# Small inputs of a one-core transformer kernel laid out by the host, and zero products ahead of the first real ones

## What is computed

```python
mod = (silu(c) @ wmod).reshape(16, 6, 1, 128)              # sa, ca, ga, sb, cb, gb
h = layernorm(x) * (1 + ca) + sa
h = sqrt(128) * h + pos
for l in range(4):
    n = layernorm(h) * ln1_s[l] + ln1_b[l]
    q, k, v = n @ Wq[l] + bq[l], n @ Wk[l] + bk[l], n @ Wv[l] + bv[l]
    h = h + linear_attention(elu(q) + 1, elu(k) + 1, v) @ Wo[l] + bo[l]
    n = layernorm(h) * ln2_s[l] + ln2_b[l]
    h = h + relu(n @ W1[l] + b1[l]) @ W2[l] + b2[l]
x = x + ga * (layernorm(h) * lnf_s + lnf_b)
x = x + gb * experts(layernorm(x) * (1 + cb) + sb)         # 8 experts, top 2, and a shared one
```

## Time and profile before

| | us |
|---|---|
| median of 3 runs | 573.39 |
| lowest, highest | 573.23, 573.44 |
| the profiled execution, its own time | 575.53 |
| its span in the profile | 573.4 |
| PE busy in the span | 555.7 (97%) |
| DVE busy | 440.4 (77%) |
| ACT busy | 394.9 (69%) |
| POOL busy | 261.4 (46%) |

### The profile page before, as it was taken

The page is one execution under the profiler, slowest core; times in us unless marked ns, Lnnn a source line. Parts: engine busy times, 40 slices in busy tenths (PEclk is TensorE's granted clock), DMA queues, the critical chain, the costliest instruction groups (busy, mean ns, idle before and its releaser), DMA issues.

```text
span 573.4 us, 13217 instructions
## 1 busy us (share of the span) xinstructions
PE 555.7 (97%) x4572; PEld 532.5 (93%) x4572; DVE 440.4 (77%) x1543; ACT 394.9 (69%) x1395; POOL 261.4 (46%) x431
## 2 busy tenths in 40 slices
PE   5899999999999999999999999999999999999997
PEld 3488899999999999998999999998999999999896
DVE  4877777778986777777997777778897667667795
ACT  2877978786666666786594765787676666666651
POOL 4344668454323446654503526646313435336420
PEclk9989999999999999999999999999999999999999
DMA  7700254000000000000000000000000000000000
GB/s 223 225 5 1 67 188 181 5 1 2 21 1 20 1 2 2 1 2 2 2 19 21 1 1 2 1 2 1 2 19 19 2 2 1 2 2 1 2 19 18
DMA packets 11049, 15.60 MB, mean 27 GB/s; under 512 B 960, under 2 KB 8224, under 8 KB 10600
## 3 DMA queue, kind: packets, MB, share of 16 engines
q1 hardware_dynamic: 8904, 12.54, 7.1%
q0 software_dynamic: 448, 1.25, 0.8%
q10 hardware_dynamic: 1632, 0.98, 0.6%
HBM read 12.63 MB, written 2.14 MB: 26 GB/s over the span
## 4 chain that ended last, share of the span: by engine, by line
PE 86%; ACT 5%; DVE 5%; POOL 1%; issue 1%; DMA 1%; DVEq 0%; SPq 0%; POOLq 0%
PE psA L1624 21%; PE psD L1624 19%; PE psB L1624 19%; PE psC L1624 19%; PE psB L1696 1%; PE psC L1696 1%; PE psD L1696 1%; PE psA L1696 1%; DMA wm<-in_wmod 1%; ACT L524 1%; ACT L478 1%; PE psA L1747 1%; PE psB L1747 1%; PE psC L1747 0%; PE psD L1747 0%
## 5 line engine op out<-in xcount | busy, mean ns | idle before, releaser
L843 POOL TENSOR_TENSOR rstdD<-msD,neghalf 128x2 f32<-128x2 f32 x20 | 14.0, 699 | 53.8 <-ACT ziD L470 41.7
L1624 PE MATMUL psC<-w,H 128*128 128x128 f32 x256 | 34.2, 276 | 0.5 <-ACT H L493 0.5
L1624 PE MATMUL psB<-w,H 128*128 128x128 f32 x256 | 33.1, 275 | 0.0
L1624 PE MATMUL psA<-w,H 128*128 128x128 f32 x256 | 33.0, 275 | 0.0
L1624 PEld LDWEIGHTS psC<-w,H 128*128 128x128 f32 x256 | 31.1, 192 | 1.5 <-ACT H L493 1.5
L1624 PE MATMUL psD<-w,H 128*128 128x128 f32 x256 | 31.8, 275 | 0.0
L1624 PEld LDWEIGHTS psB<-w,H 128*128 128x128 f32 x256 | 30.9, 192 | 0.0
L1624 PEld LDWEIGHTS psA<-w,H 128*128 128x128 f32 x256 | 30.8, 192 | 0.0
L1624 PEld LDWEIGHTS psD<-w,H 128*128 128x128 f32 x256 | 30.3, 192 | 0.0
L470 ACT ACTIVATE eqkA<-xA 128x129 f32<-128x129 f32 x64 | 19.3, 307 | 11.4 <-DVE xA L1190 10.5
L843 POOL TENSOR_TENSOR rstdA<-msA,neghalf 128x2 f32<-128x2 f32 x20 | 14.6, 732 | 26.8 <-ACT eqkA L470 23.0
(11 more groups left out here) (587 smaller groups left out, 2403.9 us busy)
## 6 DMA issues: line engine op xcount, KB each, us to landing
M<-modulation_rows SPq DMA_DIRECT2D x2, 1280.0 KB, 9.1
M<-modulation_rows SPq DMA_DIRECT2D x1, 2560.0 KB, 8.8
out<-X SPq DMA_DIRECT2D x16, 128.0 KB, 1.9
M<-in_attn_W SPq DMA_DIRECT2D x3, 256.0 KB, 3.6
X<-in_attn_x_in ACTq DMA_DIRECT2D x2, 256.0 KB, 3.6
M<-in_attn_W ACTq DMA_DIRECT2D x1, 256.0 KB, 3.7
wo<-in_attn_Wo POOLq DMA_DIRECT2D x1, 256.0 KB, 4.7
wm<-in_wmod SPq DMA_DIRECT2D x1, 256.0 KB, 4.3
```

The source lines that it names most:

```text
L843: pool.tensor_tensor(b.rstd[:, :], b.ms[:, :], neghalf[:, :], ALU.pow).then_inc(b.s_rstd.sem, 1)
L1624: return pe.matmul(o, lhsT, rhs, start=start, stop=stop)
```

## The change

The host now lays out the small inputs: the condition and the six parameter tables as one transposed table of 128 x 40 (`small`), the four biases joined, the last norm's scale and shift joined, the four weights of each layer joined to 896 columns, W2 with its partition first. The two transpositions on PE, the copy of `parT` on DVE and the waits for them go; `c_in` and `parT` are parts of `small`. PE begins with six products of a tile of zeros with itself (`idle_passes`), which write to a bank that is overwritten later. The arithmetic is otherwise the same.

```diff
+        small = sb("small", [P, BATCH + 6 * LAYERS])
+        c_in, parT = small[:, 0:BATCH], small[:, BATCH:]
...
+        w_all = last_rows[:, 0:LAYERS * (QKV + FF)].rearrange("p (l n) -> p l n", n=QKV + FF)
+        wqkv, w1 = w_all[:, :, 0:QKV], w_all[:, :, QKV:]
...
+        zeros = CD[1].att[:, 0, :]
...
         def _(sync):
-            sync.dma_start(c_in[:, :], cond).then_inc(s_k, 16)
-            sync.dma_start(K[:, 0:C_FIRST], consts[:, 0:C_FIRST]).then_inc(s_k, 16)
+            sync.dma_start(small[:, :], small_in).then_inc(s_k, 16)
             sync.dma_start(wm[:, 0:2 * D], wmod[:, 0:2 * D]).then_inc(s_wm, 16)
-            for n, a in enumerate((ln1_s, ln1_b, ln2_s, ln2_b, bo, b2)):
-                sync.dma_start(par[n * LAYERS:(n + 1) * LAYERS, :], a).then_inc(s_par, 16)
+            sync.dma_start(K[:, 0:C_FIRST], consts[:, 0:C_FIRST]).then_inc(s_ident, 16)
             sync.dma_start(cen, consts[:, C_CEN:]).then_inc(s_par, 16)
...
+            sync.dma_start(bias[:, :, :], bias_in.rearrange("(a l) n -> a l n", a=1).to_broadcast([2, LAYERS, QKV + FF]))\
+                .then_inc(s_bias, 16)
             tiles_in = x_in.rearrange("b (t p) f -> p (b t) f", p=P)
             k = CHAINS * TILES
+            sync.dma_start(Xv[:, k // 2:k, :], tiles_in[:, k // 2:k, :]).then_inc(s_xfirst[1], 16)
+            sync.dma_start(K[:, C_FIRST:C_CEN], consts[:, C_FIRST:C_CEN]).then_inc(s_pos, 16)
+            sync.dma_start(wm[:, 2 * D:], wmod[:, 2 * D:]).then_inc(s_wm2, 16)
+            sync.dma_start(lnf, lnf_in.rearrange("(a n) -> a n", a=1).to_broadcast([BATCH, 2 * D])).then_inc(s_lnf, 16)
+            for l in range(1, LAYERS):
+                sync.dma_start(w_all[:, l, :], w_in[:, l, :]).then_inc(s_weights[l], 16)
+                if l == 1:
+                    sync.dma_start(w2[:, :, :, :].rearrange("p l c n -> p (l c) n"), w2_in).then_inc(s_w2in, 16)
...
         def _(act):
             tiles_in = x_in.rearrange("b (t p) f -> p (b t) f", p=P)
-            for n in range(2):
-                k = slice(n * 2 * TILES, (n + 1) * 2 * TILES)
-                act.dma_start(Xv[:, k, :], tiles_in[:, k, :]).then_inc(s_xfirst[n], 16)
-            for n, a in enumerate((Wq, Wk, Wv)):
-                act.dma_start(wqkv[:, 0, n * D:(n + 1) * D], a[0, :, :]).then_inc(s_wqkv[0], 16)
-            act.dma_start(w1[:, 0, :], W1[0, :, :]).then_inc(s_w1[0], 16)
+            act.dma_start(Xv[:, 0:2 * TILES, :], tiles_in[:, 0:2 * TILES, :]).then_inc(s_xfirst[0], 16)
+            act.dma_start(w_all[:, 0, :], w_in[:, 0, :]).then_inc(s_weights[0], 16)
 
             def condition():
 
-                act.wait_ge(s_parps, 1)
-                act.activation(condT[:, :], A.ps[:, 1, 0:BATCH], ACT.Silu).then_inc(s_condT, 1)
+                act.wait_ge(s_k, 16)
+                act.activation(condT[:, :], c_in, ACT.Silu).then_inc(s_condT, 1)
...
         def _(pool):
+            pool.memset(zeros, 0.0).then_inc(s_zero, 1)
             pool.memset(neghalf[:, :], -0.5).then_inc(s_const, 1)
...
         def _(dve):
 
-            def parameters():
-
-                dve.wait_ge(s_parps, 2)
-                dve.tensor_copy(parT[:, :], A.ps[:, 1, 0:6 * LAYERS]).then_inc(s_parT, 1)
-                dve.wait_ge(s_parT, 1)
-
             def fold_matrix(n):
 
                 l, k = n // 2, n % 2
+                dve.wait_ge(s_k, 16)
+                dve.wait_ge(s_ident, 16)
...
-            def condition():
-
-                pe.wait_ge(s_k, 32)
-                pe.transpose(A.ps[:, 1, 0:BATCH], c_in[:, :], ident[0:BATCH, 0:BATCH]).then_inc(s_parps, 1)
-
-            def parameters():
-
-                pe.wait_ge(s_condT, 1)
-                pe.wait_ge(s_par, 112)
-                pe.transpose(A.ps[:, 1, 0:6 * LAYERS], par[:, :],
-                             ident[0:6 * LAYERS, 0:6 * LAYERS]).then_inc(s_parps, 1)
+            def idle_passes(n):
+
+                pe.wait_ge(s_zero, 1)
+                for _ in range(n):
+                    mm(D_.ps[:, 0, 0:D], zeros, zeros)
 
             def bias_rows(k):
 
                 if k == 0:
-                    pe.wait_ge(s_parT, 1)
+                    pe.wait_ge(s_k, 16)
+                    pe.wait_ge(s_par, 16)
...
-                pe.wait_ge((s_wqkv, s_w1)[k][min(l, 1)], (48, 16)[k] * (1 if l == 0 else LAYERS - 1))
-                pe.wait_ge(s_bias, 64)
+                pe.wait_ge(s_weights[l], 16)
+                pe.wait_ge(s_bias, 16)
...
-            condition()
+            idle_passes(6)
             first_rows(D_)
             first_rows(B)
             first_rows(C)
             first_rows(A)
-            parameters()
             bias_rows(0)
```

More of the change, by code:

```diff
@@ L38 @@
 ENTRY_PE = (3, 1, 2, 0)
-ENTRY_DVE = (2, 0, 1, 3)
 ROUTE_STEPS = 14
@@ L101, in of, with program @@
         return self.value(i, names.index(name) + 1)
-def program(nc, x_in, Wq, bq, Wk, bk, Wv, bv, Wo, bo, W1, b1, W2, b2, ln1_s, ln1_b, ln2_s, ln2_b, lnf_s, lnf_b,
-            router, e_gate, e_up, e_down, s_gate, s_up, s_down, cond, wmod, consts, select, out, rows):
+def program(nc, x_in, Wo, router, e_gate, e_up, e_down, s_gate, s_up, s_down, wmod, small_in, bias_in, lnf_in, w_in,
+            w2_in, consts, select, out, rows):
     nc.disable_value_cache = True
@@ L271, in program @@
         s_spread = [sem(f"spread{n}") for n in range(len(SPREAD))]
-        s_wqkv, s_w1 = [sem("wqkv"), sem("wqkvrest")], [sem("w1in"), sem("w1rest")]
+        s_weights = [sem(f"weights{l}") for l in range(LAYERS)]
         s_wo, s_w2in, s_wmoe = sem("wo"), sem("w2in"), sem("wmoe")
@@ L279, in program @@
         s_parps = sem("parps")
-        s_parT = sem("parT")
+        s_ident = sem("ident")
         s_bplus = sem("bplus")
         s_inmod = sem("inmod")
-        s_factor = sem("factor")
+        s_zero = sem("zero")
         s_condT = sem("condT")
@@ L339, in _ @@
             sync.dma_start(cen, consts[:, C_CEN:]).then_inc(s_par, 16)
-            sync.dma_start(K[:, C_FIRST:C_CEN], consts[:, C_FIRST:C_CEN]).then_inc(s_pos, 16)
-            for n, a in enumerate((bq, bk, bv)):
-                sync.dma_start(bias[:, :, n * D:(n + 1) * D],
-                               a.rearrange("(a l) n -> a l n", a=1).to_broadcast([2, LAYERS, D])).then_inc(s_bias, 16)
-            sync.dma_start(bias[:, :, QKV:], b1.rearrange("(a l) n -> a l n", a=1).to_broadcast([2, LAYERS, FF])).then_inc(s_bias, 16)
@@ L2169, in _, with laid_out @@
                     expand(B, i + 1, 0, 0)
-_INS = ["attn_x_in", "attn_Wq", "attn_bq", "attn_Wk", "attn_bk", "attn_Wv", "attn_bv", "attn_Wo", "attn_bo",
-        "attn_W1", "attn_b1", "attn_W2", "attn_b2", "attn_ln1_s", "attn_ln1_b", "attn_ln2_s", "attn_ln2_b",
-        "attn_lnf_s", "attn_lnf_b", "ffn_router", "ffn_experts_gate", "ffn_experts_up", "ffn_experts_down",
-        "ffn_shared_gate", "ffn_shared_up", "ffn_shared_down", "c", "wmod"]
+_INS = ["attn_x_in", "attn_Wo", "ffn_router", "ffn_experts_gate", "ffn_experts_up", "ffn_experts_down",
+        "ffn_shared_gate", "ffn_shared_up", "ffn_shared_down", "wmod"]
+def laid_out(get):
+    small = [get("c")] + [get("attn_" + n) for n in ("ln1_s", "ln1_b", "ln2_s", "ln2_b", "bo", "b2")]
+    w2 = get("attn_W2").reshape(LAYERS, CH, P, D).transpose(2, 0, 1, 3)
+    return {"in_small": np.concatenate(small, axis=0).T,
+            "in_biases": np.concatenate([get("attn_" + n) for n in ("bq", "bk", "bv", "b1")], axis=1),
+            "in_lnf": np.concatenate([get("attn_lnf_s"), get("attn_lnf_b")]),
+            "in_weights": np.concatenate([get("attn_" + n) for n in ("Wq", "Wk", "Wv", "W1")], axis=2).transpose(1, 0, 2),
+            "in_w2": w2.reshape(P, LAYERS * CH * D)}
 def build(nc, inputs):
@@ L2181, in build @@
         arrays["in_" + name] = np.ascontiguousarray(inputs["L0_" + name])
+    for name, a in laid_out(lambda name: inputs["L0_" + name]).items():
+        arrays[name] = np.ascontiguousarray(a)
     arrays["in_consts"] = constants()
```

34 lines of the change are left out of this document (10 added, 24 removed).

## The result

| | before | changed |
|---|---|---|
| median of 6 executions each, us | 573.89 (573.23 to 575.09) | 582.25 (578.61 to 584.05) |
| ratio to before, 95% interval | | 1.0131 (1.0106 to 1.0155) |
| profiled execution: time, span, us | 575.53, 573.4 | 581.0, 578.8 |

The changed kernel is slower: by 8.4 us by the medians, by 7.5 us by the ratio. A comparison leaves out executions that lie over 1.5% above the fastest of the same kernel, here four of the fourteen of `e9` and one of the kernel before (921.17 us, beside `e9` to `e12`).

The account below looks back on a forecast made before the run. PE, 97% busy, was taken as the bound, the gain as time off the chain ahead of about 26 us: 2.0 - 0.5 (clock) = 1.5 us off 575.53 us, 574.0 us, then 2.14 us to the median: 571.9 us, range 570.4 to 574.2 us.

Parts of the forecast that it names:

- Weights of the modulation: Start of the kernel: `wm`, moved to second on SP, lands at 4.4 to 5.2 us, so `first_rows` starts before 5.77 us.
- Removed on PE and DVE: Ahead of the first fold: two transpositions and the `parT` copy go; PE is through at 12.15 us even with low clock.
- DVE's start is the new limit: Tiles of C and D, sixth on SP, land at 6.2 to 7.0 us; first fold starts at 12.5 instead of 13.86 us.
- late-transfers rival: SP's queue: tiles land only at 7.9 us beside ACT's long rows, leaving 0.2 us of gain, 573.2 us; chance 0.12.
- The clock's term: PE's waits up to the first fold: a clock fall there costs 0 to 1.1 us, taken as 0.5 us.
- The slower rival: PE ahead of the first fold: clock stays low until past 18 us, giving 574.6 to 576.3 us; chance 0.13.
- The sum: Whole program: 2.0 us gain less 0.5 us for the clock gives 574.0 us, then 2.14 us to the median, 571.9 us.
- The rest costs nothing: Idle passes, memset of zeros, SP issues, W2's rows and new waits, mostly at the start: no cost.

Follow-up runs that it names:

- e9: Changed kernel with transfers ordered by when they are first read, tiles of C and D back on ACT; 573.01 us over all 14 executions, ratio 0.996.
- e12: Kernel before with the tiles of C and D issued late on SP and zero products in PE's later waits; 577.06 us, ratio 1.0047.
- e1: Changed kernel without its six opening zero products; 583.52 us, ratio 1.016.
- e15: Changed kernel with fourteen zero products ahead of the first fold only; 575.11 us, ratio 1.0024.
- e3: Changed kernel with zero products in two PE waits, 6 ahead of modulation(0) and 16 ahead of the first fold; 575.32 us, ratio 1.0025.
- e6: Kernel before with only late zero products (2, 2 and 5) in PE's later waits, no layout change; 573.21 us, ratio 0.9992.
- e13: e10 without the six opening zero products; 572.38 us, ratio 0.997.
- e10: e9 with late zero products (2, 2 and 5) in PE's later waits; 572.45 us, ratio 0.9975.
- e5: Changed kernel with tiles of C and D on ACT and zero products in PE's waits, both ahead of the first fold and later; 573.61 us, ratio 0.9986.
- e8: Changed kernel with layer 0's joined weights moved from ACT to SP, behind the tiles of C and D; 580.72 us, ratio 1.0114.
- e2: Changed kernel with the tiles of C and D back on ACT's queue, ahead of the joined weights; 574.64 us, ratio 1.0007.

## Why the prediction was wrong

It said 571.9 us and at most 574.2 us; 582.25 us came. By its own steps:

- *Weights of the modulation*, 4.4 to 5.2 us: right, 4.38 us. *Removed on PE and DVE*: right, the two transpositions and the copy are gone. PE was free at 10.1 us instead of 12.15 us, since the clock rose at 5.4 us and not "by 8 us". That looked like a gift; it made the wait ahead of the fold longer. It is not a condition of the fall, though: in e1 the clock rose at 8 us, and it fell all the same.
- *DVE's start is the new limit*: the mechanism was right, DVE works gapless from the tiles to `bias_plus_one`. Its size was not: the tiles landed at 7.7 us, outside 6.2 to 7.0 us and near the late-transfers rival's 7.9 us. The fold started at 13.6 us instead of 12.5 us. The estimate took the 3.2 to 4.0 us of transfers that stood second and third in SP's queue; the sixth took 4.7 us. With this step wrong and the clock up, e15, the time is 575.11 us, 1.3 us above the kernel before, and not the small gain that the rival gave; why, the fifth point says.
- ***The clock's term* is the step that failed.** It put the end of the range at 1.1 us, on the ground that the clock would be back by the second fold. The low level stayed for 10.2 us, with PE busy for 8.79 us of them, and a second stretch of 6.8 us followed; together they cost some 6 us (e15's trace against the change's). The price was there in the rows: the same four products take 2.08 us low and 1.14 us high, so 8.79 us of low work are, by estimate, some 4 us too many. I bounded the stretch by the one low stretch that the trace had (3.4 us) and by the rise 5.3 us after 10.03 us; neither says how long a fall after a wait of 3.5 us lasts. The Trainium skill, page "TensorE: Matmul & The Clock Gate", section "HAM oscillation — how this bites in real kernels", prices a low stretch at half the duration of its products. The traces agree for the first stretch: half of 8.79 us is 4.4 us, and e15 is 4.3 us ahead at `fold_weights(2)`; for both stretches the rule gives 7.8 us and the traces some 6 us. e3 and e15 keep the tiles late and fill the wait: about 7 of the 8.4 us are gone by the medians, 6.1 of 7.5 us by the ratios.
- *The slower rival* had the place (PE, between `modulation(0)` and the fold) and the sign (the clock low past 18 us: `bias_rows(1)` took 2.05 us at 18.57 us). Its 574.6 to 576.3 us were too few because it had the fold at 12.5 us, priced its two products at 2.76 us where they took 3.12 us (13.61 to 16.73 us), and had the clock high behind `fold_weights(1)`. The program was 3.3 us late at `fold_weights(2)` (30.80 against 27.54 us), then low from 32.7 us on, where before the low level had ended at 32.25 us. This second stretch lies where PE sets the time: 1.7 us more, 5.0 us in all at chain D's projection. The two traced executions end 5.5 us apart (581.0 against 575.53 us). The medians are 8.4 us apart, since before's traced execution lies 1.6 us above its median and the change's 1.25 us below.
- *The sum was made against the wrong trace.* Before's profiled execution had the clock rise at 15.3 us; e6 shows the same code with the clock up at 9.9 us and the fold at 12.35 us. I subtracted the 2.14 us to the median at the end, as if they lay elsewhere. By e6's trace they are the same microseconds as the 2.0 us of gain, and were counted twice: the forecast for the change had the first fold at 12.5 us and the first exponentials at 19.3 us, and e6, with the old layout, has them at 12.35 and 19.22 us. So without any trouble from the clock the sum should have come out near before's median, and 571.9 us had no ground. With the clock kept up in both, the layout in its best order gains about 1 us (e13's 0.997 beside e6's 0.9992, with intervals that overlap).
- *The rest costs nothing*: right for the idle passes' end (3.9 us). The second part of `wm` came 1.37 us late, which e15 shows to be free. That the idle passes may cost something by making the wait ahead of the fold longer, as in e10's trace, was not seen.

What stays open: why the second low stretch of the change is 6.8 us long and the one of before 3.4 us, after the same waits of 0.5, 0.2 and 1.4 us; why three of the change's six executions have a still lower clock than the traced one; and what makes the clock rise at 5.4 us in one execution and at 8 us in the next, with the same products ahead of it.

## To carry to other kernels

A gap on TensorE in front of the critical product costs more than its own length: price it with the time that the low clock then lasts, here 10 us and more in which products take twice as long, and not with the gap. Work that is taken away from TensorE ahead of a wait for something else gains nothing and can bring that gap about; fill it, or move forward what is waited for. A fill that is longer than the wait holds the product itself: in e5 `bias_plus_one` stood at 11.78 us and the fold started at 13.53 us. When small transfers are joined, look at what is queued behind and beside them: order each queue by the time at which its data is needed. And before a gain is added up against one traced execution that lies above the median, look where that execution lost its excess.

## What the runs showed of the hardware

- Ahead of the first fold the clock fell with waits of 3.49 us (the change), 3.25 us (e1), 2.76 us (e10) and 2.66 and 1.75 us in a row (e8), and not with 1.02 us (e13), 0.76 us (e2) and 0.53 us (e9), nor with 1.35 us ahead of `modulation(0)` in e15. It fell up to 1.6 us after the work had begun again: in e1 the fold's two products ran high (0.88 and 0.91 us), the next low.
- Once low it stayed low for 10.2 us in the change, 14 us in e2 and 23.6 us in e1, with PE busy for 8.79, 12.15 and 21.62 us of them, but for 3.4 us only in the stretch that before had the earlier trace rows. In e2 the only waits of note between 10 us and the fall at 20 us are those of 0.76 and 0.42 us.
- Zero products in PE's waits keep the clock up: with fourteen of them ahead of the fold it ran high in e15's trace (0.88 us), where without them it ran low (1.62 us). e5, e6 and e12, with the later waits filled, have no low stretch behind the first fold.
- The printed granted clock is 1.00 until the first change that is recorded, also where durations show the low level (1.06 us for the first rows in e13).
